# A state-space scan on five engines: in each step GpSimd makes the product with C before the drive

## The reference

```python
xz = tn @ W_in + b_in                      # tn: layer norm over channels
xi, z = (xz[..., :d_in], xz[..., d_in:])   # d_in = 256
xc = silu(causal_conv4(xi) + conv_b)
dbl = xc @ W_x                             # 8 columns for delta, 16 for B, 16 for C
delta = jax.nn.softplus(dr @ dt_w + dt_b)
def step(h, inputs):                       # over 64 tokens, d_state = 16
    d_t, B_t, C_t, x_t = inputs
    dA = jnp.exp(d_t[:, :, None] * A)
    h = dA * h + (d_t * x_t)[:, :, None] * B_t[:, None, :]
    y = jnp.einsum('nds,ns->nd', h, C_t)
    return (h, y)
out = ((y + xc * D) * silu(z)) @ W_out + b_out + x
```

## Time and profile before

| what | us |
|---|---|
| median of 3 runs (lowest to highest) | 9151.34 (9150.13 to 9157.04) |
| profiled execution: its time | 9160.72 |
| profiled execution: span from first to last instruction | 9158.9 |
| PE busy | 8504.2 (93%) |
| DVE busy | 8151.9 (89%) |
| ACT busy | 7618.8 (83%) |
| POOL busy | 8038.0 (88%) |
| mean granted clock of TensorE | 0.979 of full |

### The profile page before, as it was taken

How to read it: one execution, slowest core, us unless ns; L and a number is a source line. 1 busy time by engine, 2 the same in 40 slices (tenths; PEclk the granted TensorE clock), 3 DMA queues, 4 the chain that set the end, 5 groups by cost and what they waited for, 6 DMA issues and landing times. The chain is left out here.

```text
span 9158.9 us, 157541 instructions
## 1 busy us (share of the span) xinstructions
PE 8504.2 (93%) x52285; PEld 6526.3 (71%) x52285; DVE 8151.9 (89%) x8082; ACT 7618.8 (83%) x13798; POOL 8038.0 (88%) x3673
## 2 busy tenths in 40 slices
PE   6999999999999999999999999999799999999999
PEld 4666666666666666666666666666599999999788
DVE  5999999999999999999999999999799999999766
ACT  5999999999999999999999999999655555555577
POOL 4999999999999999999999999999799999999500
PEclk8999999999999999999999999999899999999999
DMA  3333433333443344343334443334301101011255
GB/s 92 117 122 127 126 122 124 126 122 123 128 125 124 121 128 127 121 126 123 125 122 124 127 124 122 126 125 124 107 31 38 37 33 38 33 38 37 90 187 177
DMA packets 675841, 982.03 MB, mean 107 GB/s; under 512 B 82761, under 2 KB 280402, under 8 KB 670930
## 3 DMA queue, kind: packets, MB, share of 16 engines
q1 hardware_dynamic: 675282, 974.98, 33.8%
HBM read 828.71 MB, written 146.04 MB: 106 GB/s over the span
## 5 line engine op out<-in xcount | busy, mean ns | idle before, releaser
L1092 POOL TENSOR_TENSOR prod<-state,c_all 128x1024 f32<-128x1024 f32 x1472 | 3477.6, 2371 | 224.1 <-DVE state L922 192.3
L922 DVE TENSOR_TENSOR_SCAN state<-decay_r,drive_r 128x1024 f32<-128x1024 f32 x1024 | 2328.9, 2274 | 244.7 <-PE drive_r L599 149.9
L1081 POOL TENSOR_TENSOR drive_d<-du,b_all 128x1024 f32<-128x1024 f32 x1024 | 2421.3, 2367 | 1.3 <-PE y_acc L612 1.2
L922 DVE TENSOR_TENSOR_SCAN state<-decay_d,drive_d 128x1024 f32<-128x1024 f32 x1024 | 2329.8, 2275 | 79.6 <-ACT decay_d L737 79.6
L612 PEld LDWEIGHTS y_acc<-ident,prod 128*128 128x128 f32 x16384 | 1894.1, 143 | 609.5 <-issue 514.1
L612 PE MATMUL y_acc<-ident,prod 128*128 128x128 f32 x16384 | 2199.3, 278 | 20.4 <-POOL prod L1092 6.4
L1369 DVE SCALAR_TENSOR_TENSOR sum_d<-bank_d,filt,sum_d 128x512 f32<-128x512 f32 x2470 | 1654.7, 743 | 119.3 <-PE bank_d L1277 119.3
L750 ACT ACTIVATE ub<-ut,bt 128x256 f32<-128x256 f32 x4096 | 1736.7, 497 | 12.7 <-issue 0.4
L1416 POOL TENSOR_TENSOR sum_p<-sum_p,scaled 128x1024 f32<-128x1024 f32 x650 | 1554.3, 2391 | 80.5 <-ACT scaled L1327 32.9
L1327 ACT ACTIVATE scaled<-bank_p,filt 128x512 f32<-128x512 f32 x1560 | 944.6, 689 | 622.3 <-PE bank_p L1277 616.0
L737 ACT ACTIVATE decay_d<-delta,neg_a 128x504 f32<-128x504 f32 x2048 | 1309.6, 671 | 39.8 <-DVE state L922 35.2
(11 more groups left out here) (156 smaller groups left out, 13497.7 us busy)
## 6 DMA issues: line engine op xcount, KB each, us to landing
c_all<-bc_rows SPq DMA_DIRECT2D x1472, 256.0 KB, 3.3
b_all<-bc_rows SPq DMA_DIRECT2D x1024, 256.0 KB, 3.7
ys<-row_spectra SPq DMA_DIRECT2D x130, 256.0 KB, 2.8
column_sums<-tt SPq DMA_DIRECT2D x130, 256.0 KB, 2.2
x_in<-in_x_dram SPq DMA_DIRECT2D x64, 512.0 KB, 4.9
x_res<-in_x_dram SPq DMA_DIRECT2D x64, 512.0 KB, 5.0
x_rows<-x SPq DMA_DIRECT2D x64, 512.0 KB, 5.1
row_spectra<-z SPq DMA_DIRECT2D x64, 512.0 KB, 4.7
```

Source lines behind the costliest of these rows:

```text
L922: dve.tensor_tensor_scan(state[place_of(ALLSTEPS, M, n, NT)][:].rearrange("p h t -> p (h t)"), decay[:].rearrange("p h w t -> p (h w t)"), ...
L1081: pool.tensor_tensor(drive_d[place_of(DSTEPS, M, n, ND)][:], du[:, :, q * HT:(q + 1) * HT], b_all[slot][:].unsqueeze(1).to_broadcast([P, 2 ...
L1092: pool.tensor_tensor(prod[place_of(ALLSTEPS, M, n, NP)][:], state[place_of(ALLSTEPS, M, n, NT)][:], c_all[slot][:].unsqueeze(1).to_broadca ...
```

## The change

In each step GpSimd now makes the product first and the drive second. What lies around the two (`others`) stays.

```diff
             def body(S, p):
                 for n in range(NSTEP):
                     others(S, p, 2 * n)
+                    if (n - 1) % NSTEP in BY_GPSIMD and S.step(n - 1, p):
+                        times_c(S.step(n - 1, p))
                     if (n + 3) % NSTEP in DSTEPS and S.step(n + 3, p):
                         make_drive(S.step(n + 3, p))
-                    if (n - 1) % NSTEP in BY_GPSIMD and S.step(n - 1, p):
-                        times_c(S.step(n - 1, p))
                     others(S, p, 2 * n + 1)
```

## The result

The change makes the kernel slower: 9240.9 us in the median (9238.1 to 9245.4), against 9154.2 for the kernel before in the same session. The ratio is 1.0096, with a 95% interval of 1.0084 to 1.0108, or +87 us. The profiled execution took 9245.4 us, its span is 9243.5. The forecast was +62 us, with a range of +9 to +104.

The account below looks back on a forecast made before the run. Bound: the block chain from step 7's delta through TensorE to turn 15, scan 15, and VectorE to the next delta. Late ut11 54 us plus late low stretches 8 us gave +62 us, 9213 us; range 9160 to 9255.

Parts of the forecast that it names:

- Only the pair of step 9 costs: GpSimd's eight swapped pairs per block: only step 9's drive, now behind product 8, delays the second du, by 2.33 us.
- ut11 late by 1.36, 0.21 and 1.21 us by kind of block, 54 us in all: TensorE's transposes of the second du start late in 25 blocks like 60, 26 like 61, 12 like 17 or odd.
- It reaches scan 15 in full: TensorE runs without a gap from ut11 to turn 15, so all the lateness reaches VectorE's scan 15.
- The rival that it is absorbed: Slack over 1.4 us in TensorE between ut11 and turn 15 hides the delay: 9151 us; chance 0.07.
- 8 us for late low stretches: Half of 25 clean blocks get a low TensorE clock late in the block: 12 x 0.67 us.
- My own upper bound: A late low stretch of TensorE's clock in every block adds 42 us to the 54: +96 us.
- the old mixture: Low stretches of TensorE's clock stay in blocks as before, since step 7's idle remains; base of the 54 us.
- The prediction's last sign: If ut11 waits and blocks take 102 us or more throughout, the assumed mixture of low stretches was wrong.
- Step 3 at nothing: GpSimd's product 3 starts 1.4 us late, lost by step 9 in the wait for scan 8; priced at nothing.
- the cover I had named: For step 3: TensorE adds a product three steps after its scan, 9.5 us on average; without it 1.4 us a block.
- The rival with 9273 us: A new low stretch follows TensorE's new idle before ut11 in 37 blocks, 60 us more; chance 0.10.
- Steps 25 and 27 give nothing: GpSimd's products 24 and 26 run 2.33 us earlier, but TensorE's weight loads found waiting need product 27, which does not move.

Follow-up runs that it names:

- e1: Changed order, product first, in step 9 alone, against the kernel before: 9244.5 us against 9153.7, ratio 1.0096.
- e8: Product first in every pair but those of steps 3 and 9, against the kernel before: 9151.0 us, ratio 1.0002.
- the doses: Kernel before, old order, second du put off by spare GpSimd work of 0.65, 1.24, 2.33 and 3.57 us: 9150.4, 9218.0, 9241.4 and 9313.0 us against 9147.2.
- e7: Product first in step 3 alone, against the kernel before: 9170.2 us against 9147.2, ratio 1.0025.
- e2: Product first everywhere but in step 9, against the kernel before: 9171.5 us against 9153.7, ratio 1.0020.
- e5: Kernel before, old order, with a spare GpSimd product of 1.24 us ahead of the second du only: 9218.0 us against 9147.2, ratio 1.0078.
- e3: Changed kernel with the second du made right behind the first (half step 19 instead of 21): 9164.0 us against 9153.7 for the kernel before, ratio 1.0009.
- e11: Kernel before with VectorE's first delta of step 7 taken ahead of scan 7: 9118.8 us against 9146.1, ratio 0.9969.

## Why the prediction was right, and what it mis-sized

- **Only the pair of step 9 costs.** Right: e1 has the whole loss, and e8 shows six of the other pairs at nothing.
- **ut11 late by 1.36, 0.21 and 1.21 us by kind of block, 54 us in all.** The stretch up to ut11 grew by 0.91 us a block, 57 us. Block 60 had ut11 at 38.20 and the sum at 38.12. The difference is the hand-over from GpSimd to TensorE, 0.15 us where I had put the 0.08 of VectorE to GpSimd. That the totals match is luck: the kinds changed. No block like 61, for 26 of which I had put 0.21 us, is left. 41 blocks have no early low stretch, with ut11 mostly at 38.20, 1.44 us later than in the short blocks before; 22 have one, with ut11 mostly at 39.65, 1.3 us later than in blocks like 17.
- **It reaches scan 15 in full.** Right, by turn 15 in block 60 and by the doses. The rival that it is absorbed is out.
- **8 us for late low stretches.** This is the term that was mis-sized: I let 12 more blocks have one, and it was 52 more, all of them. The stretch from ut11 on grew by 0.43 us a block, 27 us. My own upper bound, a late one in every block and +96 us, was close to the result of +87. Nothing in the rows of before was against it; I had taken the old mixture as nearest, and it was not. The prediction's last sign, blocks of 102 us or more throughout, nearly came true (101.80 to 103.32).
- **Step 3 at nothing.** Right only because the change also moves the drive of step 9, which lets product 8 wait for its scan. Alone it costs 23 us (e7), and not through the cover I had named: the trace of e2 shows the second du holding ut11 back by 0.16 us, and late low stretches became more frequent with it (18 blocks in e7, 11 before). Product 2's wait was 2.93 us in block 60, where I had 2.4, and product 8's 1.20.
- **No low stretch behind the new idle.** The rival with 9273 us is out: I found no block of the changed kernel with one that begins between ut11 and 70 us, but for block 0. The trace also speaks against the Trainium skill, "TensorE: Matmul & The Clock Gate", section "Part 4: PE-mode transpose", by which the full clock does not engage for transposes: from 6294.23 to 6299.18, around the new idle of block 60, TensorE does nothing but transposes, eight of them take 1.04 us on either side of it, and the granted clock stays at 1.00:

```profile
6295.00:6299.00 4.00, 2.73 (x26) 2.53 (x25) 1.99 (x3) 4.00 (x9) 4.00 (x3) 1.00 0.25 74
```

- **Steps 25 and 27 give nothing.** Right; TensorE's weight loads waited 17.6 us for products instead of 26.0, and e8 is no faster.

What stays open: why the late low stretch comes to every block at one length and to few at another. The runs show that it needs no long wait for du (50 blocks in e5; 18 in e3, where du is waited for once). That it goes by the block's length is my reading and not shown: a low stretch itself makes its block longer, so length and low stretches come together, and a run in which only the phase of the blocks was moved was not tried.

## What to carry to other kernels

When two instructions of an in-order engine are swapped, look at what is queued behind them and not only at their own readers: here all eight swapped pairs cost 8 to 10 us at most once the second du was moved up (e3), and the loss came from a third instruction that now stood behind a wait and a whole instruction. An engine's idle time before an instruction is not its slack; that is how early its result is for the reader, by kind of block (1.0 us in one, 2.2 in another). And where TensorE has a periodic idle that is sometimes followed by a low clock, a delay elsewhere can change how often it is: a late low stretch in every block made a third of this loss.

## What the runs showed of the hardware that was not expected

- A lateness of 1.24 us, of which some 0.3 us reached TensorE's ut11, cost 71 us of 9147; blocks with two low stretches of TensorE's clock (0.54 granted) became the rule: 44 of 63, where it had been 9.
- The times of such a kernel do not rise in proportion to a delay: 0.65, 1.24, 2.33 and 3.57 us gave +3, +71, +94 and +166 us.
- The idle of 2.16 us before turn11 was followed by a low stretch in 38 blocks of 63, in the same code; two idles of 1.03 and 1.30 us with 1.6 us of work between gave it in 1 of 63 (e11).
- TensorE's transposes of du began 0.14 to 0.15 us after the end of GpSimd's du in the waits for it (block 60: 6297.69 to 6297.84). GpSimd's product began 0.08 us after the end of VectorE's scan.
